# A decoder layer on one core: batch order, beta, softplus and weight splitting moved between queues

## What is computed

```
attention (16 heads of 16):  q, k = normalised rows of x@Wq, x@Wk;  v = silu(x@Wv);  beta = sigmoid(x@Wb)
    delta = (v_t - S^T k_t) * beta_t;  S = S + k_t delta^T;  o_t = S^T q_t     (256 steps per batch)
    o = rms-normalised o, @ Wo;  added to x, layer-normalised
state space (256 channels x 16 states), on the second input ctx:
    u = silu(conv4(in_proj ctx));  B, C, dt = x_proj u;  delta = softplus(dt_proj dt + bias)
    state_n = state_n * exp(delta * A_n) + delta*u*B_n;  y = sum_n state_n * C_n + D*u
    y * silu(attention result);  added, layer-normalised
experts: 2 shared and 16 routed experts of width 176 (relu MLP), routed ones gated by the top 4 of 16 scores
    out = 2*x + sum_e gate_e * expert_e(x);  layer-normalised
```

## Time and profile before

| | |
|---|---|
| median of 3 runs | 583.9 us (582.71 to 586.61) |
| the profiled execution | 587.0 us, of which span 585.2 us |
| busy: PE / DVE / ACT / POOL | 430.1 / 405.9 / 223.9 / 204.3 us |
| first scan of the state space starts | 95.4 us |
| first expert product starts | 403.5 us |
| last product of the experts ends | 575.4 us |

### The profile page before, as it was taken

One profiled execution on the slowest core, in us unless ns is written; L12 is line 12 of the kernel. 1 busy time (PEld: TensorE's weight loads), 2 busy tenths in 40 slices (PEclk: granted clock), 3 DMA queues, 4 the chain that ended last, 5 costly groups with the idle time before them and its releaser, 6 DMA issues.

```text
span 585.2 us, 18602 instructions
## 1 busy us (share of the span) xinstructions
PE 430.1 (73%) x8286; PEld 312.3 (53%) x8286; DVE 405.9 (69%) x536; ACT 223.9 (38%) x418; POOL 204.3 (35%) x117
## 2 busy tenths in 40 slices
PE   4486068886946578857665579625899999999993
PEld 2334056553635544534444555212578888888883
DVE  1643978999984689998994047999987686333336
ACT  2486075556363235357323226502152522222220
POOL 2331157869050013542114001421634354444440
PEclk9876557675975679876765559777999999999997
DMA  8767445574130014333212003752134444555402
GB/s 260 249 217 228 161 166 166 149 197 167 55 94 4 4 50 95 77 76 74 39 24 57 4 5 85 229 206 64 72 121 168 144 174 158 172 181 178 146 1 72
DMA packets 29580, 70.10 MB, mean 120 GB/s; under 512 B 4946, under 2 KB 7708, under 8 KB 29500
## 3 DMA queue, kind: packets, MB, share of 16 engines
q1 hardware_dynamic: 29339, 68.87, 37.9%
q0 software_dynamic: 160, 0.04, 0.1%
HBM read 54.54 MB, written 14.35 MB: 118 GB/s over the span
## 4 chain that ended last, share of the span: by engine, by line
PE 43%; DVE 35%; issue 14%; DMA 2%; ACT 2%; SPq 2%; POOL 1%; DVEq 1%; ACTq 0%
DVE arena_h L1345 12%; PE bank L755 10%; DVE arena_h L1354 7%; PE bank L966 4%; PE bank L943 4%; PE bank L962 4%; PE bank L963 4%; PE bank L944 4%; PE bank L945 4%; PE bank L745 3%; DMA w_hl<-in_w 2%; PE bank L948 2%; DVE tmp_o L1396 2%; SPq L566 2%; PE bank L727 1%
## 5 line engine op out<-in xcount | busy, mean ns | idle before, releaser
L687 POOL TENSOR_TENSOR arena_s<-du,bc 128x1024 f32<-128x1024 f32 x32 | 88.3, 2762 | 216.8 <-DMA bc<-scr_x 181.4
L692 POOL TENSOR_TENSOR hg_lo<-vkp,hg_hi 128x512 fp32r<-128x512 f32 x50 | 70.7, 1414 | 88.6 <-DVE hg_hi L1578 88.6
L1345 DVE TENSOR_TENSOR_SCAN arena_h<-arena_s 128x1024 f32<-128x1024 f32 x32 | 87.9, 2746 | 6.6 <-DVE arena_h L1354 4.5
L745 PE MATMUL bank<-arena_h,const 128*128 128x512 f32 x128 | 84.1, 794 | 8.6 <-DVEq L1356 8.2
L1212 ACT ACTIVATE vkp<-bank,b 128x512 f32<-128x512 f32 x50 | 34.4, 689 | 117.4 <-PE bank L945 108.3
L755 PE MATMUL bank<-vkp,tiles 32*32 32x32 f32 (+1 forms) x3072 | 44.7, 213 | 46.9 <-issue 30.2
L755 PEld LDWEIGHTS bank<-vkp,tiles 32*32 32x32 f32 x3072 | 40.8, 133 | 52.8 <-issue 33.7
L1574 DVE TENSOR_TENSOR vkp<-vkp,bank 128x512 f32<-128x512 f32 x50 | 34.3, 686 | 48.5 <-ACT vkp L1212 46.7
L1070 ACT ACTIVATE arena_s<-delta,negA 128x510 f32<-128x510 f32 x64 | 43.0, 713 | 58.5 <-DVEq L1346 57.9
L1354 DVE TENSOR_TENSOR arena_h<-arena_h,bc 128x1024 f32<-128x1024 f32 x32 | 56.6, 1768 | 12.2 <-PE bank L745 8.3
L678 POOL TENSOR_TENSOR w_hl<-w_hl 128x512 fp32r<-128x512 f32 x25 | 42.3, 1709 | 60.4 <-ACT w_hl L1205 60.4
(11 more groups left out here) (160 smaller groups left out, 742.1 us busy)
## 6 DMA issues: line engine op xcount, KB each, us to landing
w_ring<-scr_w SPq DMA_DIRECT2D x50, 512.0 KB, 3.3
bc<-scr_x SPq DMA_DIRECT2D x32, 512.0 KB, 5.0
scr_w<-w_hl SPq DMA_DIRECT2D x25, 512.0 KB, 3.0
w_hl<-in_w SPq DMA_DIRECT2D x25, 256.0 KB, 3.8
xT<-in_x_t SPq DMA_DIRECT2D x1, 1024.0 KB, 7.6
xres<-in_x_tok SPq DMA_DIRECT2D x1, 1024.0 KB, 9.7
out<-xres SPq DMA_DIRECT2D x8, 128.0 KB, 1.8
wqkvb<-in_wqkvb SPq DMA_DIRECT2D x1, 784.0 KB, 5.5
```

What stands on the lines that cost most here:

```text
L687: pool.tensor_tensor(dBu[:, i % 2, :].rearrange("p (e t) -> p e t", e=2), du[:, :, GT_ * th:GT_ * th + GT_], bc[:, i % NBC, 0, :].unsqueez ...
L692: pool.tensor_tensor(hg_lo[i % 2][:, :], hrel[:, i % 2, :], hg_hi[i % 2][:, :], ALU.subtract).then_inc(s_hglo, 1)
L745: mm = pe.matmul(o[:, :], ident, hC[i % NHC][:, GT_ * et:GT_ * et + GT_], start=(n == 0), stop=(n == DS - 1))
L1345: link(dve.tensor_tensor_scan(hst, dA[:, i % 2, :], dBu[:, i % 2, :], 0.0, ALU.mult, ALU.add))
```

## The change

- **Beta.** It is made once for all batches: PE makes 16 rows for 512 tokens at a time, ACT one sigmoid per half, SP stores it, and SP loads it spread over the partitions (eight transfers per batch) and in the form that `solve2` needs (four, as before). The keys are no longer multiplied by beta; beta takes the mask's place as the factor of the P products (L1459 before, L1528 after). The widened copy of the weights of beta goes.
- **V** is made for all four batches at the start, in four buffers.
- **Clamps.** The two clamps per batch on DVE go. A small bias in the Ln takes their place, and a minimum inside the multiplication of `kn` and `qn`. The product of `kn` is written where the P products read it; ACT copies it from there.
- **Softplus.** The four last operations of each half move from DVE to POOL; ACT makes one more (minus one) and uses Relu for the positive part.
- **Weight splitting.** `wraw` of tile g is planned after `dbu` of step g, with two buffers in place of three: one tile per step of the state space.
- **Experts.** The first two tiles of each half hold shared experts only (2*176 columns, 2 tiles of 128 are wholly theirs); they take no gate product, no multiplication and need not wait for the gates.
- **Order.** Other costs in the plan, other points at which a batch may begin (`BEGIN`), and an offset per stage that is added to the length of the way (`AHEAD`). The add of step i now also waits for the last sum of a half when it needs that buffer.

```diff
-NWS = 3
+NWS = 2
+FREE = NSH * DFF // P
 NHC = 3
 RING = 8
-HOP = 0.12
+HOP = 0.15
 NBC = 3
 BLOCK, FETCH = 256, 3.75
+BEGIN = {1: ("dve", "P3"), 2: ("act", "S1"), 3: ("act", "tile_t"), "dt": ("pe", "UW1"), "scan": ("act", "kn")}
+AHEAD = {("attention", 2): 20, ("attention", 3): 10, ("experts", 0): 20, ("experts", 1): -40, ("middle", 0): 50, ("middle", 1): 30, ("ssm", 1): 20}
...
-            k = min(open_, key=lambda k: (ways[k][0], -way[k]))
+            k = min(open_, key=lambda k: (ways[k][0], -way[k] - AHEAD.get(stage(*k[1:]), 0)))
...
-    if b % 2:
-        on = [*on, ("act", "tile_u", b - 1)]
+    if b in BEGIN:
+        on = [*on, (*BEGIN[b], b - 1)]
...
-        p = op("pe", f"P{w}", b, .8, [p, qn], takes=[(f"P{w}", b)], ins=128)
-        d = op("dve", f"P{w}", b, .6, [p, d])
+        p = op("pe", f"P{w}", b, 1.5, [p, qn], takes=[(f"P{w}", b)], ins=128)
+        d = op("dve", f"P{w}", b, .65, [p, d, beta])
...
+    p, v = None, []
+    for b in range(B):
+        p = op("pe", "v", b, 1.9, [p, xe[-1] if b > 1 else None], takes=[("v", b)], ins=16)
+        v.append(op("act", "v", b, .65, [p, silu[0]], frees=[("v", b)]))
+    p = op("pe", "b", 0, 3.6, [p], takes=[("b", 0), ("b", 1)], ins=16)
+    beta = op("act", "b", 0, 3.8, [p, *v, silu[1]], frees=[("b", 0), ("b", 1)])
+    op("sp", "beta_st", 0, .6, [beta], lag=2.6)
...
+        pe_ = op("pe", "dt", et, 2.0, [pe_, (*BEGIN["dt"], 0)], takes=[("dt", et, 0), ("dt", et, 1)])
+        act_ = op("act", "dt", et, 7.3, [pe_, dve_] if et else [pe_], frees=[("dt", et, 0), ("dt", et, 1)])
+        dve_ = op("pool", "dt", et, 10.4, [act_, kept])
...
-        r = op("sp", "wraw", g, .3, [staged[g - NWS][1]] if g >= NWS else [], lag=3.5)
+        r = op("sp", "wraw", g, .3, [staged[g - NWS][1] if g >= NWS else None, ("pool", "dbu", g)], lag=3.5)
...
-        scan[i] = op("dve", "scan", i, 2.4, [decay, dbu[i], add.get(i - 1)])
+        scan[i] = op("dve", "scan", i, 2.4, [decay, dbu[i], (*BEGIN["scan"], 0) if i == 0 else None, add.get(i - 1)])
...
-            def move_b(b):
+            def keep_beta():
+                sp.wait_ge(s_sig, NG)
+                for th in range(NG):
+                    for half in range(2):
+                        sp.dma_start(scr_b[GB * th:GB * th + GB, :, L * half:L * half + L].rearrange("b h l -> h b l"),
+                                     at_g[th][HH * half:HH * half + HH, :].rearrange("h (b l) -> h b l", b=GB)).then_inc(s_bst, 16)
+
+            def spread_beta(b):
                 x, n = b % 2, b // 2
-                sp.wait_ge(s_beta[x], n + 1)
-                sp.dma_start(scr_b[b], beta_kc[x][0:P:DH, :]).then_inc(s_bdram[x], 16)
-                sp.wait_ge(s_bdram[x], 16 * (n + 1))
+                if b == 0:
+                    sp.wait_ge(s_bst, 16 * 4)
+                if n:
+                    sp.wait_ge(s_at[x], 4 * n)
+                    sp.wait_ge(s_turned[x], n)
+                for h in range(HH):
+                    sp.dma_start(beta_kc[x][DH * h:DH * h + DH, :], scr_b[b, h, :].partition_broadcast(DH)).then_inc(s_beta[x], 16)
...
+            def softplus(et):
+
+                pool.wait_ge(s_sp, et + 1)
+                link(pool.tensor_tensor(sp_w, sp_w, sp_z, ALU.subtract))
+                link(pool.tensor_tensor(sp_l, sp_l, sp_w, ALU.subtract))
+                link(pool.tensor_tensor(delta[:, et, :], delta[:, et, :], sp_l, ALU.add))
+                pool.nop().then_inc(s_spf, 1)
+                pool.nop().then_inc(s_delta, 1)
+                if et == 0:
+                    pool.wait_ge(s_xkept, 16)
+                pool.tensor_tensor(du[:, et, :], delta[:, et, :], u[:, et, :], ALU.mult).then_inc(s_du, 1)
...
+            def betas():
+                pe.wait_ge(s_ld_c, LD_C)
+                for th in range(NG):
+                    k = ("b", th)
+                    o = fill(k)
+                    for kt in range(KT):
+                        mm = pe.matmul(o[0:H, :], wqkvb[:, kt, 3 * D:3 * D + H], xT[:, kt, GT_ * th:GT_ * th + GT_],
+                                       start=(kt == 0), stop=(kt == KT - 1))
...
                 if ft == 0:
                     pe.wait_ge(s_xlo, th + 1)
+                if ft == FREE:
...
-                filled(k, pe.matmul(fill(k)[:, :], sel[:, P * ft:P * ft + P], gstk[th], start=True, stop=True))
+                if ft >= FREE:
+                    filled(k, pe.matmul(fill(k)[:, :], sel[:, P * ft:P * ft + P], gstk[th], start=True, stop=True))
...
+            def betas():
+                for th in range(NG):
+                    k = ("b", th)
+                    signal(act.activation(at_g[th][0:H, :], take(k)[0:H, :], ACT.Sigmoid), s_sig, th + 1, k)
+                nc.scalar.preload_act_table_set(LN_EXP)
...
-                act.activation(sp_l, sp_w, ACT.Ln).then_inc(s_sp, 1)
+                link(act.activation(sp_l, sp_w, ACT.Ln))
+                act.activation(sp_w, sp_w, ACT.Identity, bias=bias_col(BI_LESS)).then_inc(s_sp, 1)
...
-                    link(act.activation(r, r, ACT.Ln, scale=float(2 ** SCALE_LOG2)))
+                    link(act.activation(r, o[:, :], ACT.Ln, scale=float(2 ** SCALE_LOG2), bias=bias_col(BI_TINY)))
+                    free(k)
                     act.activation(r, r, ACT.Exp, scale=-0.5,
...
+                if i >= NHC:
+                    th, n = divmod(i - NHC, DS)
+                    if n < DS - 1:
+                        dve.wait_ge(s_summed, i - NHC + 1 - th)
+                    else:
+                        for et in range(2):
+                            take(("ysum", th, et))
...
-                if name in ("ssk", "ssq"):
-                    signal(dve.tensor_scalar(r, take(k)[:, :], 1e-24, None, ALU.max),
-                           s_clamp[x], 2 * n + (name == "ssq") + 1, k)
-                if name == "kn":
-                    k = ("k", b)
+                                  v_w[b][:, :].rearrange("p (c h n) -> p c h n", c=NC, h=2)).then_inc(s_vc[x], 1)
+                if name in ("kn", "qn"):
+                    is_q = name == "qn"
+                    k = (name[0], b)
                     o = take(k)
-                    dve.wait_ge(s_rs[x], 2 * n + 1)
-                    signal(dve.tensor_tensor(k_uv[x][:, :], o[:, :], r, ALU.mult),
-                           s_k[x], n + 1, k)
-                    dve.wait_ge(s_beta[x], n + 1)
-                    link(dve.tensor_tensor(qke[x][:, :, :, C:2 * C], hcn(k_uv[x][:, :]), hcn(beta_kc[x][:, :]), ALU.mult))
...
+                    signal(dve.scalar_tensor_tensor(out=flat(qke[x]).rearrange("p (m w) -> p m w", w=W3)[:, :, at:at + C],
+                                                    in0=tmp_o[x][:, :].rearrange("p (m n) -> p m n", n=C), scalar=0.25e12 if is_q else 1e12,
+                                                    in1=o[:, :].rearrange("p (m n) -> p m n", n=C), op0=ALU.min, op1=ALU.mult),
+                           s_qk[x] if is_q else s_k[x], n + 1, k)
...
+                    dve.wait_ge(s_beta[x], 16 * HH * (n + 1))
                     dve.tensor_tensor(hcn(at_g[x][:, :])[:, half, cs, :], o[:, :, C:2 * C],
-                                      mask_a.unsqueeze(1).broadcast_to([P, CH, C]), ALU.mult).then_inc(s_at[x], 1)
+                                      hcn(beta_kc[x][:, :])[:, half, cs, :], ALU.mult).then_inc(s_at[x], 1)
```

215 lines of the change are left out of this document (109 added, 106 removed).

## The result

The changed kernel takes 566.68 us (median of 4 runs, 562.22 to 568.51), the kernel before, run beside it, 585.25 (582.71 to 587.27). The ratio is 0.9663 with a 95% interval of 0.9608 to 0.9719. Forecast were 567, range 546 to 593. The profiled execution took 568.51 (span 566.7). Ratios leave out a run that took over 1.5% more than the fastest of its kernel.

A forecast was written before the change was run, and what follows sets the result against it. DVE's work ahead of the gated experts, then PE's experts, then a tail bound it: 118 + 224 + 40 + 20 = 402; 402 + 158 + 8.4 = 568.4 span; plus 1.8, less 3.1: 567 us, range 546 to 593.

The forecast's parts named there:

- 1. First scan: First scan moves from 95.4 to 118 us (bounds 112 to 127), now behind the solve and UW of batch 1.
- 2. DVE's own work: DVE's own work from the first scan to the gates: 224 us, against 237.2 before.
- 3. Meetings: POOL's work stops DVE between first scan and gates: 107 us of POOL at 0.37 give 40 us, 30 before.
- rival B: POOL's meetings with DVE cost 0.6 us per us of POOL, 64 us and not 40: 591 us; chance 0.08.
- 4. Waits: DVE's waits from first scan to gates: 20 us (bounds 0 and 40.5); the 15.9 us at `yT` go.
- 5. Experts: PE's expert phase behind the gates: 48 tiles at 3.05 us plus the rest, together 158.0 us.
- 6. Tail: Tail after the experts: 8.4 us, 9.8 less 1.38 for the first half's normalisation, now made during the experts.
- Rival A: The lists fit and DVE waits for PE 5 us in all, not 20: 552 us; chance 0.14.
- E: The waits only move: DVE waits as long as before, 40.5 us, giving 587 us; chance 0.13.
- C: Weight-splitting chain over two buffers: late tiles stop scans, 2 us for each of 13 pairs, 593 us; chance 0.05.
- D: PE's stalls grow in batches 2 and 3: 3.4 us more for ten blocks, 601 us; chance 0.07.

The follow-up runs named there:

- the fills: The change with three write-only fills of an unread buffer (128x512) on POOL ahead of each split: 573.41 us, 0.9829 of the kernel before.
- A doubled split: The change with each of the 25 splits on POOL made twice, first into an unread buffer: 583.28 us, 0.9945 of the kernel before.
- the two halves: The change's operations in an order made from the old kernel's durations: 591.21 us; the old kernel's operations in an order made from the new durations: 612.03 us.

## Why the prediction came out

The mechanism was right: DVE's work ahead of the gates and PE's experts behind them set the time, and each term of the sum is found in the profile. That the time was right to 0.3 us is luck. Four errors of 5 to 11 us cancelled on the way to the gates, and a second measurement of the same kernel gave 2.8 us less. The profiled span, 566.7, stands against a forecast of 568.4; the step from there to the median, for which 3.1 us were taken off, measured 1.8.

*1. First scan:* 112.70, forecast 118 (112 to 127). The first solve ended at 62.3, not 66: the stall in the P products of batch 0 is 0.53 us (5.17 before, under 3 forecast), in a stretch whose DMA share fell as foreseen, to 0.28 between 40 and 73 us (0.59 before). The two clamps of batch 0 were priced at their own 1.4 us; putting clamps back moved the end of this solve by 3.6. That and the 4.6 us of stall are 8.2 of the 10.2 us by which it came earlier; the rest isn't traced. The softplus meetings were 8.0 us, forecast 7. POOL's first dbu was ready 2.8 us late, forecast as hidden.

*2. DVE's own work:* 291.0 - 45.6 - 31 = 214.4, forecast 224. Too high by 9.4. The small waits and gaps in it are 19.1 us, 25.7 before, of which the forecast took off by name only the clamps' 1 us; this is more than half of the error. What the rest is stays open, and some other operations were stretched by meetings too and count in the 214.4.

*3. Meetings:* 45.6, forecast 40; 0.43 us per us of POOL's unhindered 107, forecast 0.37. In the change's other profile the excess is 46.4. The mean scan, 3.27 (3.18 there), is not near the 2.75 that I had named as a sign but at the 3.2 of rival B; the add, 1.67, is far under B's 2.3. B decided from 0.53 on and is out. The mechanism, exclusion, was shown by the fills and by the one-for-one rows above. The price per us was the wrong kind of number: it was a mean over one arrangement. A doubled split added little stretching and much lateness.

The Trainium skill, "SBUF — State Buffer", section "Who interferes with whom", says that a VectorE instruction with two SBUF inputs contends with a GpSimd instruction that reads SBUF, not with one that only writes it. The trace agrees in both: 2.35 us for a product of 100 elements beside a subtraction or product of POOL, and DVE less busy, not more, with 75 fills (39.2 us) on POOL.

*4. Waits:* about 31, forecast 20; those for PE alone 28.2, over the 15 to 25 that I had named. The wait at `yT` went, as forecast. The add of step 24 waits 8.51, forecast 7 for this place; `on` 3.0, forecast 2. Not foreseen were the adds of 12 (2.65), 19 (2.33) and 23 (3.61).

The first gated tile: 403.74 (398.4 in the other profile), forecast 402, from errors of -5.3, -9.4, +5.6 and +11.

*5. Experts:* 154.4, forecast 158.0. 48 x 3.05 = 146.4 leaves 8.0 for the rest, forecast 11.9. About 1.1 us of that is the start: PE's first seven products of the stretch took 2.8 us before and take 1.7 now. Where the other 2.8 went is open. Ahead of the gates PE stood 6.2 us, not some 12. That the ungated tiles gain by filling PE's stand is shown (7.4 us when the first half's two are gated again; two tiles at 3.05 are 6.1).

*6. Tail:* 8.55, forecast 8.4.

Rival A (waits of 5 us) and E (40) are both refuted by the 31. C did not happen, though its sign as written (POOL waiting over 15 us for ACT's rounding) was met: POOL waited 26.3 us, but DVE only 2.8 for POOL. The sign was badly chosen, since POOL has time to wait. C's mechanism is real and was produced by moving six tiles. For D, PE stood 55.2 us in 25 pieces for nothing that the profile shows (54.3 in 30 before), with 139 GB/s beside it instead of 84. In sum it did not grow, but D's sign, stalls over 3 us among the small products, was met: five pieces are over 4 us, the longest

```profile
253.60 0.55 PE L831 MATMUL bank<-vkp,tiles 32*32 32x32 f32 x24 [5.57 <-issue]
```

where the kernel before had one of 4.05. The stretch also holds fewer small products, 4932 against 5997, so a product carries 11.2 ns of stall against 9.1. In the change's other profile it is 45.9 us for 5017, 9.1 ns again, and none among the small products is over 3.7. Whether D grew a little is thus not decided by two profiles; that it didn't cost the 34 us of the rival is. The forecast did not say that the two halves of the change need each other; the sum went by the combined lists, so it did not have to, but a reader who took "fewer operations" or "better order" as separate gains would have been wrong by about 25 us: 591 and 612 were measured for the two halves.

## What to carry to other kernels

Where two engines meet at a deadline, compare what has been done by then and not the time of the deadline: here it didn't move, and the gain is in what no longer lies behind it. Take operations off the chain ahead of the bound stretch first; four of 0.7 us were worth 8.5 there, with their handovers, and four in the stretch too little to be seen. Make the order anew for each change of the operations, look in each in-order list for the one step that waits for a slow transfer with urgent steps behind it, and don't expect halves of a change to add up.

## What was not expected of the hardware

A scan of 128x1024 takes mostly one of few lengths, 2.3, 3.1 or 4.1 to 4.4 us; the longest is 2.29 and nearly the whole of a dbu beside it. Blocking goes by whole operations, so a mean such as 0.4 us per us says little about the next one.

Fills by POOL of 128x512 (0.52 us each) leave DVE's adds alone (1.22 us beside three of them), while a subtraction of the same size stops a scan (3.15 for 2.29). The clock granted to PE in the attention stretch was 0.71 before and 0.73 after (a mean over pieces at 0.50 and at 1.00, which are 1.2 and 2.4 GHz) with 55 GB/s more traffic beside it; neither the traffic nor the order moved it visibly.
